# Last attention group split in two halves of queries, and two chunks of its output projection moved into the first FFN

## The reference

```python
x = x + _layernorm(attn(_layernorm(x), Wq, Wkv, Wo, bo))        # 32 heads of 16, 8 groups of keys and values, causal
x = x + _layernorm(ffn0(_layernorm(x)))                          # ternary weights: silu(x gate.T) * (x up.T), then down.T
x = x + _layernorm(autocorrelation(_layernorm(x)))               # FFT along the row, top 6 lags, softmax of them, weighted rolls
x = x + _layernorm(ffn1(_layernorm(x)))                          # gate, up and down with LoRA terms
```

```python
weights = softmax(where(causal, -inf, q k.T) / 4)                # per head
ctx = weights v                                                  # b, t, (h d): 1024 x 512
return ctx Wo + bo
```

## Time and profile before

| what | value |
|---|---|
| median of 3 runs | 874.64 us (870.46 to 874.67) |
| the profiled execution's own time | 875.61 us |
| its span, first to last instruction | 873.9 us |
| mean granted clock of PE | 0.938 of full |
| busy: PE, DVE, ACT, POOL | 86%, 71%, 41%, 34% of the span |

### The profile page before, as it was taken

How to read it: one execution, slowest core, us unless ns; L and a number is a source line. 1 busy time by engine, 2 the same in 40 slices (tenths; PEclk the granted TensorE clock), 3 DMA queues, 4 the chain that set the end, 5 groups by cost and what they waited for, 6 DMA issues and landing times.

```text
span 873.9 us, 15737 instructions
## 1 busy us (share of the span) xinstructions
PE 747.3 (86%) x5385; PEld 431.1 (49%) x5406; DVE 620.2 (71%) x1294; ACT 361.6 (41%) x699; POOL 294.8 (34%) x350
## 2 busy tenths in 40 slices
PE   0966855999799999998896999799989999899994
PEld 0722422333233333332334767476757867667773
DVE  7613765766657677689289999996889786796713
ACT  1212222565556656576502443534453343443231
POOL 4022445012121212213212555445645324334431
PEclk9988766899989999998998999899999999999998
DMA  9399798861814313265352259263484231110100
GB/s 278 58 178 297 247 245 224 176 125 31 134 32 96 75 31 50 54 163 172 110 181 58 58 91 254 63 148 68 66 144 93 29 58 25 26 50 1 49 26 24
DMA packets 145003, 93.63 MB, mean 107 GB/s; under 512 B 112360, under 2 KB 123496, under 8 KB 144728
## 3 DMA queue, kind: packets, MB, share of 16 engines
q1 hardware_dynamic: 133888, 70.45, 36.7%
q10 hardware_dynamic: 10816, 16.91, 6.4%
q0 software_dynamic: 240, 5.51, 3.0%
HBM read 48.73 MB, written 29.04 MB: 89 GB/s over the span
## 4 chain that ended last, share of the span: by engine, by line
PE 55%; DMA 12%; DVE 12%; SPq 6%; issue 5%; ACT 5%; POOL 4%; DVEq 0%; ACTq 0%; POOLq 0%
PE ps L1206 18%; PE ps L1504 9%; PE ps L1228 9%; PE ps L1468 6%; PE ps L1481 6%; PE ps L1184 4%; DMA lorad_d<-arena 2%; ACT arena L1443 2%; SPq L395 2%; DMA qp_d<-arena 2%; DMA arena<-in_L_ffn_up_w_dram 2%; DMA arena<-qp_d 2%; DMA arena<-arena 1%; DVE mx L1358 1%; DMA lora_d<-arena 1%
## 5 line engine op out<-in xcount | busy, mean ns | idle before, releaser
L1206 PE MATMUL ps<-arena 128*128 128x256 f16 (+1 forms) x1952 | 235.0, 277 | 6.6 <-DMA arena<-arena 6.6
L1206 PEld LDWEIGHTS ps<-arena 128*128 128x128 f16 (+1 forms) x1952 | 195.3, 101 | 49.4 <-issue 8.5
L1443 ACT ACTIVATE arena<-ps 128x1024 f32<-128x1024 f32 (+7 forms) x256 | 161.9, 651 | 111.5 <-PE ps L1481 105.0
L1358 DVE TENSOR_REDUCE mx<-ps 128x1 f32<-128x512 f32 (+1 forms) x256 | 158.8, 654 | 54.8 <-PE ps L1471 27.7
L1057 POOL TENSOR_TENSOR arena<-arena 128x256 f32<-128x256 f32 (+1 forms) x100 | 82.5, 825 | 233.6 <-ACT arena L948 233.0
L1468 PE MATMUL ps<-arena 96*128 (+4 forms) x384 | 133.6, 364 | 28.4 <-DVE mx L1358 8.9
L1228 PE MATMUL ps<-arena 128*128 128x512 f16 (+2 forms) x467 | 119.1, 384 | 16.9 <-POOL arena L1063 15.3
L1481 PE MATMUL ps<-arena 99*128 (+4 forms) x384 | 126.1, 342 | 8.2 <-ACT arena L1443 7.8
L1341 POOL TENSOR_SCALAR_AFFINE_SELECT arena<-arena 128x512 f32<-128x512 f32 x64 | 42.0, 657 | 216.2 <-ACT arena L1443 216.2
L1504 PE MATMUL ps<-arena 128*32 128x256 f32 (+1 forms) x1280 | 97.9, 378 | 3.7 <-POOL arena L1341 2.3
L1468 PEld LDWEIGHTS ps<-arena 96*128 (+1 forms) x384 | 39.3, 103 | 115.6 <-issue 73.8
(11 more groups left out here) (157 smaller groups left out, 852.1 us busy)
## 6 DMA issues: line engine op xcount, KB each, us to landing
arena<-qp_d SPq DMA_DIRECT2D x48, 128.0 KB, 5.0
lora_d<-arena ACTq DMA_DIRECT2D x20, 256.0 KB, 3.9
arena<-lora_d SPq DMA_DIRECT2D x10, 512.0 KB, 5.0
w1n_d<-arena SPq DMA_DIRECT2D x10, 512.0 KB, 3.8
arena<-rec_d SPq DMA_DIRECT2D x32, 128.0 KB, 2.6
qp_d<-arena SPq DMA_DIRECT2D x12, 256.0 KB, 4.1
w1dn_d<-arena SPq DMA_DIRECT2D x4, 704.0 KB, 4.1
arena<-in_L_ffn_down_w_dram ACTq DMA_DIRECT2D x16, 172.0 KB, 3.5
```

The lines of the kernel that those rows point to most:

```text
L1206: last = nc.tensor.matmul(ps[0:h, b, CH * o:CH * (o + 1)], w(t[0])[:, kt, ht * P:ht * P + h], xt[:, c, t[1], kt, :], start=(kt, t) == (0, ...
L1358: nc.vector.reduce_max(to[:, h, t:t + 1], s_bank(g, u)[:, 0:w], mybir.AxisListType.X).then_inc(s_taken, 1)
L1443: nc.scalar.activation(probs[:, kt % 2, h, kt * P:T], st_bank(h).rearrange("p b n -> p (b n)")[:, kt * P:T], ACT.Exp, scale=HD ** -0.5).th ...
```

## The change

1. **The last group's queries 0 to 511.** They are complete after key step 3. DVE copies them out (last_group_taken), a matmul with a selecting matrix (spread, one for each chunk) puts each head's sum on all its rows, DVE takes the reciprocal and multiplies (last_group_normalised), and the result is used as it lies, against a copy of the last 64 rows of Wo with zeros in between (wo7). A row tile of chunks 0 and 1 so has 5 matmuls.
2. **Projection of chunk 0** is done within the last group, in pieces behind key steps 3, 5, 6 and 7, and that of chunk 1 behind it. The normalisation of group 6 is moved from step 4 to step 2.
3. **Projection of chunks 2 and 3** stands ahead of tiles 3 and 13 of the first FFN (late_out). The hops for the last group's other half go on beside that, with POOL's multiplication at tile 2.
4. **DVE's order:** hidden_tiles(6, 7) go behind after_attention(0), prepare_down(0) behind after_attention(3), prepare_down(2) ahead of the first spectra, the last ffn_pieces ahead of spectra(2).
5. **SP's order:** the bias row for chunk 3 is loaded behind the second long transpose, down_store(0) behind the transposes of chunk 3.
6. **Tables** of the third layer.

```diff
-        CORR_AT = (29, 48, 65, 76)
-        SPEC_AT = (38, 58, 69, 80)
+        CORR_AT = (32, 52, 65, 77)
+        SPEC_AT = (37, 59, 69, 80)
-        LAGS_AT = (29, 54, 66, 77)
-        WTAKE_AT = (39, 58, 69, 80)
+        LAGS_AT = (32, 54, 66, 77)
+        WTAKE_AT = (40, 59, 72, 80)
...
         def sp_rest(sp):
+            den_hop(sp, G - 1, 0)
+            den_hop(sp, G - 1, 1)
+            hidden_store(sp, 4, 8)
+            hidden_store(sp, 5, 9)
             transposes(sp, "attn", 0)
-            sp.wait_ge(o_ready, SUB * NCH)
-            sp.dma_start(row_late, ...).then_inc(late_row_loaded, 16)
+            den_hop(sp, G - 1, 2)
+            den_hop(sp, G - 1, 3)
+            ctx_store(sp, G - 1, 1, T // 2)
...
             transposes(sp, "ffn", 0)
-            down_store(sp, 0)
             sp.dma_start(inv_sb[1], inverse[1]).then_inc(inverse_loaded, 16)
             w1_transpose(sp, w1g[:, 1], 1, 0)
+            sp.wait_ge(o_ready, SUB * NCH)
+            sp.dma_start(row_late, ...).then_inc(late_row_loaded, 16)
             transposes(sp, "attn", 3)
+            down_store(sp, 0)
...
+        def last_group_taken(dve, c):
+            dve.wait_ge(pv_done, NT * (G - 1) + NT // 2)
+            nc.vector.tensor_copy(o7[c], o_flat[:, CH * c:CH * (c + 1)]).then_inc(o7_taken, 1)
+        def last_group_normalised(dve, c):
+            dve.wait_ge(d7_ready, c + 1)
+            nc.vector.reciprocal(r7[c], ps[:, D7_BANK[c], 0:CH]).then_inc(r7_ready, 1)
+            dve.wait_ge(r7_ready, c + 1)
+            nc.vector.tensor_tensor(o7[c], o7[c], r7[c], ALU.mult).then_inc(o7_ready, 1)
...
         def dve_rest(dve, link):
             after_attention(dve, link, 0)
+            reciprocals(dve, G - 1)
+            hidden_tiles(dve, range(6, 8))
...
             after_ffn(dve, link, 0)
-            prepare_down(dve, link, 0)
             dve.wait_ge(late_row_loaded, 16)
             after_attention(dve, link, 3)
+            prepare_down(dve, link, 0)
             peaks(dve, link, 0)
...
-        OUT_BANK = (4, 6, 4, 2)
+        OUT_BANK = ((0, 1), (4, 2), (3, 5), (2, 3))
+        D7_BANK = (1, 2)
...
+        def late_out(pe, c):
+            for i in range(SUB):
+                if c == 3:
+                    pe.wait_ge(o_free, SUB * 2 + i)
+                out_rows(c, i, [(kt, P) for kt in range(ND - 1)])
+                if (c, i) == (2, 0):
+                    pe.wait_ge(ctx_stored_last, 16 * REP)
+                out_rows(c, i, [(ND - 1, P)]).then_inc(o_ready, 1)
...
+                if shape == G - 1 and kt == 3:
+                    early_out(pe, 0, 0)
+                if shape == G - 1 and kt == 5:
+                    spread(pe, 0)
+                if shape == G - 1 and kt == 6:
+                    early_out(pe, 0, 1)
+                    spread(pe, 1)
+                if shape == G - 1 and kt == 7:
+                    early_out_end(pe, 0, 0)
+                    early_out_end(pe, 0, 1)
```

More of the change, by code:

```diff
@@ L848, in dve_rest @@
             after_ffn(dve, link, 1)
+            prepare_down(dve, link, 2)
             spectra(dve, link, 0)
-            prepare_down(dve, link, 2)
             prepare_down(dve, link, 3)
@@ L1079, in lora_job, with out_rows @@
                              lora_at[0:QROWS, A_AT[m] + j * w:A_AT[m] + (j + 1) * w], start=True, stop=True).then_inc(lora_ready, 1)
-        OUT_BANK = (4, 6, 4, 2)
+        OUT_BANK = ((0, 1), (4, 2), (3, 5), (2, 3))
+        D7_BANK = (1, 2)
+        def out_rows(c, i, parts):
+            for kt, n in parts:
+                rows = slice((SUB * c + i) * P, (SUB * c + i + 1) * P)
+                if kt is None:
+                    lhs, rhs = o7[c][:, i * P:(i + 1) * P], wo7
+                else:
+                    lhs, rhs = ctxt[0:n, kt, rows], wo[0:n, kt, :]
+                last = nc.tensor.matmul(ps[:, OUT_BANK[c][i], :], lhs, rhs, start=kt == 0, stop=kt is None or (c > 1 and kt == ND - 1))
+            return last
@@ L1083, in pe_rest @@
         def pe_rest(pe):
[L1085 to L1086 removed]
+            for i in range(SUB):
+                early_out(pe, 1, i)
+            for i in range(SUB):
+                early_out_end(pe, 1, i)
             pe.wait_ge(p_ready, 32 * G)
[L1089 to L1093 removed]
@@ L1107, in pe_rest @@
-            for i in range(SUB):
-                out_rows(3, i, [ND - 1]).then_inc(o_ready, 1)
             for i in range(3):
@@ L1122, in pe_rest @@
                         back(pe, c)
+                for c in range(2, NCH):
+                    if n == OUT_AT[c - 2]:
+                        late_out(pe, c)
                 pe_hidden(pe, n)
@@ L1327, in normalise @@
         def normalise(pool, g):
+            t0 = T // 2 if isinstance(g, int) and g == G - 1 else 0
             pool.wait_ge(rec_loaded, 16 * REP * (g + 1))
@@ L1411, in reciprocals @@
                 dve.wait_ge(rec_stored, 16 * g)
-            nc.vector.reciprocal(recs[:, :], dens[:, :]).then_inc(rec_ready, 1)
+            w = 16 if isinstance(g, int) and g == G - 1 else 32
+            nc.vector.reciprocal(recs[:, 0:w], dens[:, 0:w]).then_inc(rec_ready, 1)
         def dve_group(dve, g, shape):
@@ L1644, in _ @@
                                         ALU.subtract, ALU.mult).then_inc(xn_ready, 1)
+            dve.wait_ge(ident_ready, 1)
+            for h in range(REP):
+                at = 32 * h + HD
+                nc.vector.tensor_scalar(sel[:, 32 * h:32 * h + 32], ident[:, 0:32], 0.0, ident[:, at:at + 1], ALU.mult, ALU.add).then_inc(sel_ready, 1)
             lora_pieces(dve, link)
```

137 lines of the change are left out of this document (81 added, 56 removed).

## The result

| | before | after |
|---|---|---|
| median of the runs | 874.17 us (870.46 to 874.67) | 893.44 us (890.12 to 898.96) |
| ratio | | 1.0246, 95% interval 1.0189 to 1.0302 |
| profiled execution: span | 873.9 us | 897.2 us |
| mean granted clock of PE | 0.938 | 0.932 |
| busy: PE, DVE, ACT, POOL | 86%, 71%, 41%, 34% | 84%, 69%, 40%, 33% |

The change makes the kernel slower: by 2.5% in the ratio, by 2.2% (19.3 us) in the two medians, by 23.3 us in the two spans. All four engines are busy for a smaller share: what came in is mostly waiting.

The account below looks back on a forecast made before the run. PE, busy 86% and otherwise waiting for chains, was taken as the bound. The balance ran +5.5, +10.8, +17.8, then +1.2 and -3.3 to +15.7 us on 875.6, giving 891.3, put at 890; range 875 to 897.

Parts of the forecast that it names:

- The bias row: Ahead of chunk 3's bias on DVE: row issued behind a long transpose at 545.8, DVE idle 13.2 us until 549.4.
- Peaks to tile 31: From DVE's peaks, done at 578.6, to PE's pe_down of tile 31 at 584.4, 8.2 us later than before.
- the clock's 2.6: Behind PE's wait at tile 31: a low clock adds 2.6 us, making the balance +10.8.
- Start of the FFN: First FFN on PE begins at 456.1, 10.3 us earlier, with DVE deciding through chunk 0's normalisation.
- Reciprocal: DVE's reciprocal on 256 columns in the last group: 1.7 us each, from 6.0 ns a column.
- Late projection: Chunks 2 and 3 inside the first FFN on PE: 14.0 us of matmuls plus a 1.8 us wait.
- Weights' spectrum: Chunk 0 at tile 37 on PE: transposes at 596.8, landed 601.3; wait 5.6 and clock 1.4, balance +17.8.
- Behind it: After chunk 0's weights' spectrum: +17.8 carried along, 1.2 added at BACK_AT 74, 3.3 given back at chunk 3; +15.7.
- the correlation of chunk 3: Third layer, chunk 3: correlation no longer right behind its spectrum, DVE's 3.24 us wait goes, PE's weights' spectrum 3.3 sooner.
- the tables: CORR_AT and LAGS_AT three tiles later: the 2.4 us wait goes, with 7.8 us of cover for the later chain.

Follow-up runs that it names:

- e10: The kernel before with only the bias row's load moved to its late place behind the second long transpose; ratio 1.0141.
- e1: The changed kernel with the bias row's load issued ahead of both long weight transposes; ratio 1.0147 to the kernel before.
- e2: The changed kernel with the last group's first reciprocal and product ahead of weight tile 4 on DVE; ratio 1.0210 to the kernel before.
- e4: The changed kernel with the old tables and orders, keeping the early normalisation and late projection; ratio 1.0236 to the kernel before.
- e7: e5 and e6 together, with the bias row early; ratio 1.0063 to the kernel before.
- e3: The kernel before with only the schedule half: new tables, prepare_down(0) and down_store(0) later, two swaps at the spectra; ratio 1.0086.
- e9: e7 with the last group's reciprocals ahead of weight tiles 4 and 5, tile 5 behind chunk 0's normalisation, chunk 2's last projection part at tile 6; ratio 1.0049.
- e11: e9 with the schedule of the kernel before (tables, first down preparation and store, order around the spectra); ratio 1.0048.
- e5: e1 with chunk 0's correlation ahead of tile 30 instead of 32 and ACT's exponentials ahead of 31; ratio 1.0141 to the kernel before.
- e6: e1 with three of the four parts of chunk 2's projection ahead of the first FFN; ratio 1.0140 to the kernel before.
- e12: e11 with chunk 0's first FFN output transposes ahead of the first long weight transpose on SP's queue; ratio 1.0035 to the kernel before.

## Why the prediction was right, point by point

The time was right: 890 predicted, 893.4 measured. The path that decides was right too, the row behind the transposes; several terms were off and partly cancelled, and that the total came so close is in part luck. The sum's steps, in their order in the kernel's time where one rests on another:

- **The bias row.** Right in place and cause, and near in size. The step read: issued at 545.8 behind a transpose, landed at 549.4, DVE idle 13.2. It was issued at 548.39, DVE went on at 552.45 and had been idle for 11.9; the transpose held the queue for 5.54 and not 7.21. e10 gives its price without anything else, 12.8 us behind y(0); e1 takes it out, for about 9.
- **Peaks to tile 31.** The sum had 8.2 us, with the clock's 2.6 on top. The same pe_down came 9.9 later (10.9 from the common zero), with a wait of 7.4 where 8 to 9 were expected. Here luck helped: y(0) was 5.4 us later than in the sum (10.9 for 5.5), and at tile 31, before the clock's part, 2.7 of these were gone, 1.7 of them by the shorter transpose.
- **Start of the FFN.** Mis-sized. I had 10.3 us; e1, e2 and e4 show 7.4 to 7.6, the profiled changed kernel 3.1. The term that was missing is the low clock behind PE's wait for the reciprocal. I had expected that wait (2, measured 1.80) and had charged a low clock behind others, but not here. Where the clock stayed up behind the same wait, in e7, DVE nearly runs through as I had it (waits of 0.29 and 0.23) and the FFN begins 9.4 us earlier than before. In e1, with six records in 4.68 us for 3.04, DVE waits 0.84 for the second spread and 1.01 for PE's first row tile; in the changed kernel, with 5.78, it waits 2.46 and 3.36. Another 0.7 lies between the bias addition and the FFN (18.4 in e1 for 17.6).
- **Reciprocal.** 1.7 us from two narrow rows, 1.75 and 1.76 measured. By the rule of the Trainium skill ("VectorE: DVE Perf Modes", section "First, the fixed hardware budget"), as I had read its repeat count of 8, it would have been 2.8: the trace doesn't bear this reading out.
- **Late projection.** 14.0 + 1.8 = 15.8 us. From the FFN's start to y(0) the kernel before takes 45.8 us and e1, e2 and e4 take 58.9 to 59.2, so 13.3, a wait of 1.5 included (12 if e3's or e10's stretch, 47.2 and 46.8, stands for the kernel before). This and the start's error nearly cancel, which is luck: +5.5 predicted at y(0), 5.7 to 5.9 in these three. The profiled changed kernel had 10.9.
- **Weights' spectrum.** Its transposes were put at 596.8, the spectrum at 601.3; they came at 599.89 and 604.41. The long transpose held 8.86 instead of 8.1, and prepare_down(1) waited 1.83 for its load.
- **Behind it.** The balance was to stay at +17.8 and give back 3.3 at chunk 3. The rows spectrum of chunk 1 is 23.9 later (636.53 against 612.65), for two waits of 1.95 and 1.41 that no term had; the last pe_down is 22.9 later (883.67 against 860.73). Both are counted from the spans' starts; from the common zero each is 1.0 more. The one that I had predicted to be gained, the correlation of chunk 3, is without a wait, but 1.47 and 2.11 stand close behind it. So "holds nothing that is later than PE by this sum" was wrong by some 3 us, and of the gain about 1 came.
- **What I took for a part of the bargain, and wasn't:** the tables. I had given them cover of 7.8 us. e3 prices them at 5.6 us on the kernel before, with chunk 3 on time; with it late, e4 measures no price. e9 and e11 don't differ either, but in e9 the correlation had been moved from tile 32 back to 30.

In sum: from the common zero the profiled execution ends 24.3 us later, and I had 15.7. Of the 8.6 between, half stood there when PE came to tile 37 (22.1 later, I had 17.8), half came behind it. Against the medians the sum does better (19.3 us), since that execution lay 5.5 us over its own median. The low clock behind the reciprocal is of that kind: its FFN begins at 44.7, that of e7, whose clock stayed up, at 38.4.

## What to carry to other kernels

Moving a transfer in an in-order queue is an edit of its own: ask what stands ahead of it now, how long that holds the queue, and which engine waits for it in order. Here one load of a row, moved behind two long transposes, cost 12.8 us, about what the matmuls of two chunks of projection take (14.0). If work is moved so that a chain may begin sooner, look at which engine the chain runs on: a start 11.5 us earlier on PE was worth nothing at y(0), because DVE had 81.4 us of work up to there in place of 70.5, and stood idle for 14.1 us around the start of the stretch, where it had prepared weight tiles before. And a table of steps fits one arrival time: change what it was set for, and try the old one again.

## What the hardware showed that I had not expected

- **The clock after the same wait.** PE's wait for the first reciprocal was 1.80 us each time. Behind it, six records took 5.78 us in the changed kernel (granted clock 0.51 over 430 to 437 us, thus almost all at 1.2 GHz, and 0.62 over 437 to 446), 4.68 in e1, e5 and e6, 4.51 in e4, and 3.04 in e7, whose granted clock stayed at 1.00. The instructions of the last group ahead of it were the same. PE's timeline of e7:

```profile
433.38 3.04 PE L1128 MATMUL ps<-arena 128*128 128x512 f32 x6 [1.80 <-DVE arena L860]
```

- **The scatter of the early part.** The common zero lies between 410.6 and 420.1 us in the fourteen kernels, which are alike or nearly so up to there. That is over 1% of the run, as much as many of the effects here; without a common zero e1 would read as a gain of 17.5 us instead of 12.5.
- **How long a long transpose holds the queue.** The first one held it for 8.60 to 10.63 us in thirteen of the fourteen kernels, and for 7.04 in e12, where it stands behind the small transposes; the second held it for 5.42 to 7.74, the third (in front of the lags' transposes) for 8.06 to 10.60.
